# Graph network kernel: where the edge rows are kept, and when they are sent to memory

## What is computed

```python
x = layernorm(x + L0(x))   # two rounds of  segment_sum((x @ W)[src], dst) + b, relu between
x = layernorm(x + L1(x))   # e = silu(silu([h[row], h[col], dist] @ eW1 + eb1) @ eW2 + eb2)
                           # agg = segment_sum(e, row); out = silu([h, agg] @ nW1 + nb1) @ nW2 + nb2
x = layernorm(x + L2(x))   # agg = segment_sum([h_x[dst], h_e, h_mu[dst]], src); relu(agg @ W4.T) ...
x = layernorm(x + L3(x))   # 11 terms W[k], each step h_k = -(h - segment_sum(norm * h[col], row))
```

## Time and profile before

| | us |
|---|---|
| median of 3 runs | 1738.2 |
| the runs | 1737.69 to 1739.01 |
| profiled execution, its own time | 1737.73 |
| its span in the trace | 1735.7 |
| table stage, about | 207 to 250 |
| count stage, about | 250 to 409 |

### The profile page before, as it was taken

The page is one execution under the profiler, slowest core; times in us unless marked ns, Lnnn a source line. Parts: engine busy times, 40 slices in busy tenths (PEclk is TensorE's granted clock), DMA queues, the critical chain, the costliest instruction groups (busy, mean ns, idle before and its releaser), DMA issues. The chain is left out here.

```text
span 1735.7 us, 43832 instructions
## 1 busy us (share of the span) xinstructions
PE 1461.2 (84%) x16295; PEld 1351.0 (78%) x16295; DVE 1141.1 (66%) x3435; ACT 481.9 (28%) x910; POOL 44.6 (3%) x64
## 2 busy tenths in 40 slices
PE   0845428996997999999999969689999999999993
PEld 0534316776997788888888858679999999999993
DVE  5999837884436455555555547667767677676775
ACT  0269718993102343443434321000000000000000
POOL 1100000000000000000000012000000000000000
PEclk9978759997999999999999989889999999999996
DMA  1000014442001644445232233000000000000000
GB/s 20 7 0 0 0 28 139 133 144 75 2 2 39 167 116 133 130 115 149 70 104 69 69 83 82 6 1 2 2 3 2 3 2 2 3 2 3 2 2 21
DMA packets 36999, 83.92 MB, mean 48 GB/s; under 512 B 22926, under 2 KB 23942, under 8 KB 36848
## 3 DMA queue, kind: packets, MB, share of 16 engines
q1 hardware_dynamic: 32216, 74.42, 15.1%
q10 hardware_dynamic: 4410, 7.43, 1.7%
q0 software_dynamic: 224, 0.13, 0.0%
HBM read 60.76 MB, written 21.14 MB: 47 GB/s over the span
## 5 line engine op out<-in xcount | busy, mean ns | idle before, releaser
L1705 PE MATMUL L_psA<-L_parts,mat 125*128 125x192 bf16 x6250 | 517.2, 246 | 0.0
L1705 PEld LDWEIGHTS L_psA<-L_parts,mat 125*128 125x128 bf16 x6250 | 515.5, 98 | 1.1 <-DVE L_parts L1783 1.0
L1174 PEld LDWEIGHTS L_ps_pre<-L_drow,mat 128*128 128x128 bf16 x2250 | 128.5, 98 | 30.3 <-issue 1.1
L1340 DVE TENSOR_TENSOR L_e<-L_ps_z,L_eb 128x512 f32<-128x512 f32 x76 | 52.5, 691 | 132.7 <-PE L_ps_z L1184 132.5
L1770 DVE TENSOR_REDUCE L_sumr<-L_psA 125x64 f32<-125x192 f32 x250 | 89.4, 358 | 76.4 <-PE L_psA L1705 74.2
L1174 PE MATMUL L_ps_pre<-L_drow,mat 128*128 128x32 bf16 (+3 forms) x2250 | 132.8, 212 | 0.0
L659 DVE TENSOR_TENSOR onehot<-iota_bf,codes 128x1024 bf16<-128x1024 bf16 x150 | 98.7, 686 | 29.8 <-PE ps_extra L722 23.0
L771 PE MATMUL L_psA<-L_gparts,mat 125*128 125x192 bf16 x1250 | 112.6, 253 | 4.5 <-DVE L_gparts L784 4.5
L1647 ACT COPY L_wk<-L_Wk 128x64 f32 (+1 forms) x10 | 2.0, 242 | 404.5 <-PE L_psA L1705 404.5
L771 PEld LDWEIGHTS L_psA<-L_gparts,mat 125*128 125x128 bf16 x1250 | 108.8, 102 | 5.5 <-DVE L_gparts L784 4.8
L1168 PE MATMUL L_ps_pre<-mat,L_pp 125*128 125x512 bf16 x375 | 102.9, 383 | 2.5 <-DVE L_pp L1306 2.5
(11 more groups left out here) (296 smaller groups left out, 2365.4 us busy)
## 6 DMA issues: line engine op xcount, KB each, us to landing
L_drow<-rows_d SPq DMA_DIRECT2D x25, 728.0 KB
m_d<-panel SPq DMA_DIRECT2D x25, 684.2 KB
mat<-rows_d SPq DMA_DIRECT2D x25, 640.0 KB, 4.3
mat<-m_d SPq DMA_DIRECT2D x16, 684.2 KB
mat<-m_d ACTq DMA_DIRECT2D x9, 684.2 KB
L_drow<-rows_d SPq DMA_DIRECT2D x25, 84.5 KB
m_d<-panel SPq DMA_DIRECT2D x25, 79.4 KB
mat<-m_d SPq DMA_DIRECT2D x16, 79.4 KB
```

The lines of the kernel that those rows point to most:

```text
L1174: last = nc.tensor.matmul(ps_pre[bank][:, to:to + n], w, drow[k][:, of:of + n], start=False, stop=(r == 2 and cc == pieces[-1][0]))
L1340: nc.vector.tensor_tensor(grp(e2_of(k, g)), grp(ps_z2[bank]), eb2[:].unsqueeze(1).broadcast_to([P, len(tiles), H]), ALU.add).then_inc(bias ...
L1705: last = nc.tensor.matmul(ps[:, 0:3 * D], t.mat[0:B, kb, b * B:b * B + P], parts[src][:, kb].rearrange("p r d -> p (r d)"), start=(kb == 0 ...
```

## The change

The stage's own buffer `row_sb` goes. ScalarE copies the transposed rows to the memory of `t.xa` (seen as bf16 rows, 25 columns), and the last column by a copy of its own to the memory of `t.wsum`. The table stage has no work for SyncE any more. The 41 transfers stand in the count stage: SyncE issues the loads of the first layer's weights and `xb`, gives `stored` by hand, issues the 5 first transfers and the one of the last column, and then, for the blocks 0 to 12 written out one by one, the panel's store, and after the stores of blocks 0 to 9 two groups of the pieces (3 pieces behind an even block, 4 behind an odd one). After block 12 it waits for `rows_out` and loads the two parts of `xT`, which use the same memory; blocks 13 to 24 stay a loop. GpSimd's zeroing of the unused rows of `xT` waits for `rows_out` too.

```diff
-        row_sb = sb("row_sb", [B, NC, P], BF16)
...
-                    nc.scalar.copy(row_sb[p, lo:hi, :], ps[g][p, 0:hi - lo, :]).then_inc(row_out, 1)
+                    nc.scalar.copy(t.rows[p, lo:last, :], ps[g][p, 0:last - lo, :])
+                nc.scalar.copy(t.over_rows, ps[3][0:B, NB - held[3][0], :])
-            @block.sync
-            def _(sp):
...
-                sp.wait_ge(rows_out, 16 * 41)
...
@@ count_matrices, gpsimd
                 pool.wait_ge(padded, 1)
+                pool.wait_ge(rows_out, ROWS_OUT)
                 for rows in (l0.W1[D:B], l0.W2[D:P], l0.xT[0][D:B], l0.xT[1][D:B]):
...
@@ count_matrices, sync
                 sp.dma_start(t.xb[:], a["x"].rearrange("(b p) d -> p b d", p=B)).then_inc(l0.x_in, 16)
-                for g in range(2):
-                    load_xT(sp, a, l0, g)
-                for k in range(2):
-                    sp.sem_inc(stored[k], 32)
...
+                def send_rows(u, m):
+
+                    some, cut = slice(u * NB + m, (u + 1) * NB, 4), STEP * m % P
+                    sp.dma_start(main[u, m:NB:4, 5:NB, 0:P - cut], t.rows[some, 5:NB, cut:P]).then_inc(rows_out, 16)
+                    if cut:
+                        sp.dma_start(main[u, m:NB:4, 5:NB, P - cut:P], t.rows[some, 5:NB, 0:cut]
+                                     ).then_inc(rows_out, 16)
...
-                in_pairs(sp, NB, body)
+                for k in range(2):
+                    sp.sem_inc(stored[k], 32)
+                for u in range(5):
+                    sp.dma_start(main[u, 0:ST, 0:5], t.rows[u * ST:(u + 1) * ST, 0:5, :]).then_inc(rows_out, 16)
+                sp.dma_start(blocks[NB:5 * NB, NB, :], t.over_rows[NB:5 * NB]).then_inc(rows_out, 16)
+                for b in range(13):
+                    body(b, b % 2)
+                    if b < 10:
+                        for m in range(2):
+                            send_rows(b // 2, 2 * (b % 2) + m)
+                sp.wait_ge(rows_out, ROWS_OUT)
+                for g in range(2):
+                    load_xT(sp, a, l0, g)
+                pairs(sp, 13, NB, body)
...
+        t.rows = t.xa[:].rearrange("p b d -> p (b d)").bitcast(BF16).rearrange("p (i r) -> p i r", r=P)
+        t.over_rows = t.wsum[:].rearrange("p b w -> p (b w)").bitcast(BF16)[:, 0:P]
```

More of the change, by code:

```diff
@@ L448, in _, with edge_tables @@
                 keep_slots(NB - 1, 0)
-def edge_tables(nc, c, t, slots, rows_d):
+def edge_tables(nc, c, t, slots):
     with ExitStack() as s:
@@ L461, in edge_tables @@
         tab = sb("tab", [P, 4, NC, NB], BF16)
-        done, overs, packed, tabbed, pool_tabbed, rowed, row_out, rows_out = map(sem, (
-            "table_step", "overs", "packed", "tabbed", "pool_tabbed", "rowed", "row_out", "rows_out"))
+        done, overs, packed, tabbed, pool_tabbed, rowed = map(sem, (
+            "table_step", "overs", "packed", "tabbed", "pool_tabbed", "rowed"))
         held = ((0, 5), (5, 13), (13, 21), (21, NC))
@@ L529, in _ @@
                 for g, (lo, hi) in enumerate(held):
-                    p = slice(0, 5 * ST if g == 0 else B)
+                    p, last = slice(0, 5 * ST if g == 0 else B), min(hi, NB)
                     act.wait_ge(rowed, g + 1)
-                    nc.scalar.copy(row_sb[p, lo:hi, :], ps[g][p, 0:hi - lo, :]).then_inc(row_out, 1)
-            @block.sync
-            def _(sp):
[L536 to L550, removed]
-                sp.wait_ge(rows_out, 16 * 41)
+                    nc.scalar.copy(t.rows[p, lo:last, :], ps[g][p, 0:last - lo, :])
+                nc.scalar.copy(t.over_rows, ps[3][0:B, NB - held[3][0], :])
 def l0_inputs(nc, ctx, t):
@@ L592, in load_l1_weights, with count_matrices @@
         sp.dma_start(out_, in_).then_inc(w.w_in, 16)
-def count_matrices(nc, a, c, t, m2_d, l0):
+def count_matrices(nc, a, c, t, m2_d, rows_d, l0):
     with ExitStack() as s:
@@ L614, in count_matrices @@
         stored = [sem("panel0_stored"), sem("panel1_stored")]
-        padded, staged, hot_ready, counted, moved, added, wdone = map(sem, (
-            "padded", "codes_staged", "onehots_ready", "counted", "blocks_moved", "extras_added", "w_summed"))
+        padded, staged, hot_ready, counted, moved, added, wdone, rows_out = map(sem, (
+            "padded", "codes_staged", "onehots_ready", "counted", "blocks_moved", "extras_added", "w_summed",
+            "rows_out"))
+        ROWS_OUT = 16 * 41
         src1 = t.src1[:].rearrange("p (c b) -> p c b", b=NB)
@@ L753, in _ @@
                 sp.dma_start(t.xb[:], a["x"].rearrange("(b p) d -> p b d", p=B)).then_inc(l0.x_in, 16)
-                for g in range(2):
-                    load_xT(sp, a, l0, g)
-                for k in range(2):
-                    sp.sem_inc(stored[k], 32)
+                blocks = rows_d.rearrange("(q c r) -> q c r", c=NC, r=P)
+                main = rows_d.rearrange("(n u c r) -> u c n r", u=5, c=NC, r=P)
+                def send_rows(u, m):
[4 more added lines that the diff above has]
+                                     ).then_inc(rows_out, 16)
                 def body(b, k):
@@ L2243, in program @@
                 place_edges(nc, a, c, t)
-                edge_tables(nc, c, t, slots, rows_d)
+                edge_tables(nc, c, t, slots)
             placed = nc.values_load(c.placed_i[0:1, 0:1], min_val=0, max_val=E)
@@ L2252, in program @@
                             l0 = l0_inputs(nc, early, t)
-                            count_matrices(nc, a, c, t, m2_d, l0)
+                            count_matrices(nc, a, c, t, m2_d, rows_d, l0)
                             right.close()
```

## The result

| | us |
|---|---|
| before, median of 4 runs | 1737.95 |
| changed, median of 4 runs | 1712.86 (1711.83 to 1715.99) |
| ratio | 0.9858, 95% interval 0.9841 to 0.9875 |
| forecast | 1713.5, range 1710.0 to 1718.5 |

The account below looks back on a forecast made before the run. Bounds: TensorE's L1705 in the chain, SyncE's serial transfers ahead of the table stage's barrier, ScalarE in the count stage. 1737.73 - 24.4 (barrier) - 0.3 (stall) = 1713.0, on the median 1713.5 us; range 1710 to 1718.5.

Parts of the forecast that it names:

- The barrier, 24.4 us: Barrier behind the table stage: without SyncE's issues VectorE arrives last, at 224.87 instead of 249.27; 24.4 us off.
- the very limit that the prediction set: Barrier behind the table stage: the forecast counts as wrong if it opens later than 225.5 us.
- The copies, nothing: Table stage: ScalarE's further small copy costs under 0.84 us, ending near 219.9, still 5 us ahead of VectorE; cost nothing.
- The stall keeps its length and moves: Start of count stage: ScalarE's stall moves from ahead of block 1 to ahead of block 2; 0.3 us off.
- the bound of 1.1: Start of count stage: at best 1.1 us off, if ScalarE sees store 0 at 269.8.
- The pieces, nothing: Count stage, between stores: store and pieces take SyncE at most 4.1 us in a block of 5.72; term 0.
- The first rival: Count stage: pieces held until the store ahead has moved its data, costing 5.6 us, 1719.1 us; chance 0.13.
- Both points against it: Count stage: a store's second half was not held; over a microsecond of `xb`'s small packets fits ahead of a new transfer.
- The stall disappears: Start of count stage: row transfers not held behind `xb`, block 2 5.5 us earlier than before, 1708.3 us; chance 0.06.
- Slower than before: Count stage: each piece holds SyncE until landed, a block takes 12.1 us, 64 us more, 1777 us; chance 0.02.

Follow-up runs that it names:

- experiment 3: The changed kernel, with SyncE also issuing the 41 transfers in the table stage, to a spare buffer nobody reads, and waiting for them before the barrier; 1736.14 us.
- Experiments 1: The kernel before, with SyncE giving `stored` right behind the issue of `xb`, ahead of the two `xT` loads; 1735.59 us, ratio 0.9997.
- 2: The changed kernel, with `stored` given by hand only behind the six row transfers; 1714.64 us, ratio 0.9868.
- 6: The changed kernel, with the load of `xb` cut into five parts, issued behind the stores of blocks 10 to 14; 1707.63 us, ratio 0.9827.
- 7: The changed kernel, with the whole of `xb` loaded in one piece behind the store of block 14; 1712.88 us, ratio 0.9848.
- Experiment 5: The changed kernel, with each of the 35 pieces sent a second time, to a spare buffer nobody reads; 1721.28 us, ratio 0.9912.
- Experiment 4: The changed kernel, with all 35 pieces issued ahead of the first store instead of between the stores; 1741.77 us, ratio 1.002.

## Why the prediction was right, step by step

- *The barrier, 24.4 us.* Right. By the trace 24.5 us, counted from the start of the table stage, opened by VectorE; experiment 3 takes it back alone. No engine entered the stage less smoothly: from drain to GpSimd's first instruction it was 0.7 us and is 0.6. VectorE drained at 225.5, at the very limit that the prediction set; in the second trace of the changed kernel, which came to the table stage at 207.52, it drained at 217.1 + 7.80 = 224.9, as forecast.
- *The copies, nothing.* Right. ScalarE was done 5.7 us ahead of VectorE.
- *The stall keeps its length and moves.* Right, and it was the step that could have cost most: whoever adds the 5.60 us of rows 7 to the barrier's term forecasts 1708. Experiments 1 and 2 show both sides of it, 6 and 7 its cause. Forecast was block 2 at 20.6 us behind GpSimd's first instruction (270.6 - 249.97); measured 246.24 - 226.12 = 20.1. The term was forecast at 0.3 us and came out at 0.8: store 0 was issued at 15.8 us and not 16.5. Some 0.6 of these 0.7 us is a step that the prediction did not have. It left SyncE's way into the stage as it was, but SyncE, no longer the last at the barrier, issued `xb` 2.72 us behind GpSimd's first instruction and not 3.34. In experiment 3, where it is the last again, it is 3.3 again. The hold itself kept its length, 10.5 us for 10.66. A further 0.3 us came in blocks 3 and 4; no run shows why. With it the stage gave 1.15 us, 0.05 past the bound of 1.1.
- *The pieces, nothing.* Right. ScalarE had no wait for a store behind block 2, and pieces took 0.73 to 0.95 us. Experiment 5 gives the price beyond the cover, 4 the price without it.
- *The first rival*, pieces held behind stores, falls: no piece went over 1.3 us, though one right behind a store takes up to 0.95 where the median was 0.76. Both points against it pointed the right way; that a microsecond of small packets fits ahead of a new transfer (rows 10) was tested by no run. The Trainium skill's rule (DMA: Bandwidth & Descriptors, section on why a DMA increments its semaphore by 16) puts a transfer of 6 or 7 partitions on 6 or 7 engines. No run here splits the load by engine, so it is neither confirmed nor contradicted; the price that it seemed to speak for did not come, not even with 8 pieces behind a store.
- *The stall disappears* did not happen by itself; it happened when `xb` was moved, at about the 5.5 us that the rival gave (4.9 by the medians, 6.1 to 6.3 by the count stage).
- *Slower than before* falls with its mechanism. No piece held SyncE until it had landed, in no run. Experiment 4 is slower than before for another reason: 35 pieces at their plain issue time stand ahead of the first store. With that order the whole gain is lost, though the pieces are as quick as ever.

The sum was 24.7 us off, and the spans differ by 25.3: the barrier gave 24.5 for 24.4, the count stage 1.15 for 0.3, the stages behind it 0.3 for 0, and the late arrival at the table stage, which was no part of the forecast, takes 0.63 back. The forecast stood 0.6 us over the median. That it came so near is in part luck: the stages behind and the start of the table stage scatter by several us from trace to trace, and SyncE's quicker entry was missing. What the traces bear out is the two terms, 24.5 for 24.4 and 1.15 for 0.3.

## What to carry to other kernels

An idle stretch in which one sequencer issues small transfers ahead of a barrier is worth its whole length, if the same transfers fit between the stores of a later stage that another engine bounds; count the issue time a block has left, and put nothing ahead of the first store that someone waits for. A stall behind a semaphore that is given late is not a gain until the next wait on the same chain has been looked at: here 5.6 us moved one block on. The transfer that was worth moving stood in plain view, a load of many small packets at the head of the queue; cut into parts and sent later, it gave 5 us more.

## What was not expected of the hardware

- The load `xb`, 3125 rows of 256 bytes, held the next issue of the same queue for some 10.7 us at the start of the stage, and made ScalarE wait again where it stood in the middle. From 253.5 to 264.5 us of the trace before, while it moved, the trace has 2916 packets of 0.74 MB, all but one under 512 bytes, at 90 GB/s.
- A fifth of it in a block held the next issue by 1.6 us and made no computing engine wait.
- Stores of 764 KB hold what is issued behind them by 0.95 us at most for a piece, against a median of 0.76, while `xb`, of the same 0.8 MB, held one for 10.5. Nor is it that one is a load and the other a store: the first `xT` load, 187.5 KB in rows of 3000 bytes, let the second through (1.93 us for both), where a fifth of `xb`, with fewer bytes, held it by 1.6. So the bytes do not set the hold, but the packets' number or size, which no run tells apart.
- An engine that is no longer the last at a barrier can also be quicker behind it: SyncE by 0.6 us here.
- A large load issued by GpSimd took it 3.83 us and slowed two of VectorE's copies beside it from 0.21 to 2.00 and 1.94 us.
